# A mixture-of-experts attention stage: deviation by a square root on ScalarE, residual through TensorE, experts' scores on all partitions

## The reference

```
t = transpose(x, (1, 0, 2))                    # the 32 batch entries are the tokens here: s_len = 32
scores = softmax(t @ Wg)                       # over the 16 experts
idx = top_k(scores over the 32, cap = 32 // 16 = 2)      # two tokens of each column for each expert
hg = gather(t, idx)
q, k, v = hg @ Wq + bq, hg @ Wkv + bkv         # heads of 64
att = (q . k) / 8                              # 2 x 2 scores for each of the 256 columns
p = softmax(att, axis=1)                       # over the 256 columns
ao = (p . v) @ Wo + bo
outs = zeros.at[tokens].add(ao)
y = t + outs
yn = (y - mean) * rsqrt(var + 1e-5) * ln_g + ln_b
x = layernorm(x + yn)                          # the decoder's own residual and norm
```

## Time and profile before

| | |
|---|---|
| median of 3 runs | 3803.97 us (3803.84 to 3806.27) |
| the profiled execution | 3800.63 us |
| its span, first to last instruction | 3797.8 us |
| busy, share of the span | TensorE 87%, VectorE 82%, ScalarE 74%, GpSimd 68% |
| mean granted clock of TensorE | 0.95 of 2.4 GHz |
| stage "route" | about 821 to 924 us |
| stage "expert" | 924 to 1054 us |
| stage "scatter" | 1054 to 1204 us, next stage from 1212 us |

### The profile page before, as it was taken

The page is one execution under the profiler, slowest core; times in us unless marked ns, Lnnn a source line. Parts: engine busy times, 40 slices in busy tenths (PEclk is TensorE's granted clock), DMA queues, the critical chain, the costliest instruction groups (busy, mean ns, idle before and its releaser), DMA issues. The chain is left out here.

```text
span 3797.8 us, 75246 instructions
## 1 busy us (share of the span) xinstructions
PE 3290.3 (87%) x23328; PEld 2494.5 (66%) x23360; DVE 3118.3 (82%) x5163; ACT 2817.2 (74%) x5141; POOL 2567.5 (68%) x2971
## 2 busy tenths in 40 slices
PE   8996988979963688999988989898899879997887
PEld 5664666668542477777767777777777757775565
DVE  5665999955386699999899989989999849998887
ACT  2222777854475799899898998989899737776887
POOL 1222767730086599888888988898898936665676
PEclk9998999979976899999999999999999989998999
DMA  2112222242213111121111211111111112322111
GB/s 61 55 55 56 44 53 49 50 106 46 52 34 85 37 52 57 50 54 53 54 53 56 57 50 57 49 53 56 55 52 51 48 47 68 77 54 64 51 61 45
DMA packets 285549, 209.62 MB, mean 55 GB/s; under 512 B 131416, under 2 KB 249752, under 8 KB 285224
## 3 DMA queue, kind: packets, MB, share of 16 engines
q1 hardware_dynamic: 285224, 205.72, 19.9%
HBM read 149.18 MB, written 51.41 MB: 53 GB/s over the span
## 5 line engine op out<-in xcount | busy, mean ns | idle before, releaser
L2896 POOL TENSOR_TENSOR ma_ch<-ma_h,ma_crep 128x512 f32<-128x512 f32 x1024 | 1348.2, 1340 | 190.5 <-DVE ma_h L3007 159.8
L3007 DVE TENSOR_TENSOR_SCAN ma_h<-ma_a,ma_pbu 128x512 f32<-128x512 f32 x1024 | 1196.5, 1203 | 123.5 <-PE ma_pbu L2576 108.1
L2576 PE MATMUL ma_pbu<-ma_ident,ma_bu 128*128 128x128 f32 x4096 | 655.6, 284 | 120.6 <-DVE ma_h L3007 92.6
L2576 PEld LDWEIGHTS ma_pbu<-ma_ident,ma_bu 128*128 128x128 f32 x4096 | 481.5, 144 | 349.2 <-DVE ma_h L3007 204.3
L2785 ACT ACTIVATE ma_a<-ma_dt,ma_A 128x510 f32<-128x510 f32 x1024 | 672.8, 711 | 1.3 <-issue 1.3
L2585 PE MATMUL ma_py<-ma_ident,ma_ch 128*128 128x128 f32 x4096 | 623.9, 278 | 9.8 <-DVE ma_gT L3025 7.8
L2778 ACT ACTIVATE ma_bu<-ma_uT,ma_b_t 128x512 f32<-128x512 f32 x864 | 555.6, 711 | 13.0 <-PE ma_pbu L2576 11.3
L2585 PEld LDWEIGHTS ma_py<-ma_ident,ma_ch 128*128 128x128 f32 x4096 | 493.4, 145 | 14.3 <-DVE ma_gT L3025 11.4
L1576 POOL TENSOR_TENSOR xa_prob<-xa_e,xa_rec_head 128x616 f32<-128x616 f32 x128 | 155.6, 1217 | 126.4 <-DVE xa_rec_head L1668 114.2
L924 POOL TENSOR_TENSOR xa_prob<-xa_e,xa_rec_head 128x616 f32<-128x616 f32 x128 | 155.7, 1217 | 107.0 <-DVE xa_rec_head L1016 90.4
L362 POOL TENSOR_TENSOR la_veps<-la_mv,la_eps 128x2 f32<-128x2 f32 x32 | 6.3, 196 | 248.8 <-DVE la_mv L395 248.8
(11 more groups left out here) (375 smaller groups left out, 7942.3 us busy)
## 6 DMA issues: line engine op xcount, KB each, us to landing
ma_crep<-ma_ct_dram SPq DMA_DIRECT2D x256, 256.0 KB
xa_x<-act SPq DMA_DIRECT2D x64, 256.0 KB, 2.7
act<-xa_y SPq DMA_DIRECT2D x64, 256.0 KB, 2.2
la_x<-in_x SPq DMA_DIRECT2D x32, 256.0 KB, 2.8
act<-la_y SPq DMA_DIRECT2D x32, 256.0 KB
act<-ea_x SPq DMA_DIRECT2D x32, 256.0 KB, 4.0
ma_x<-act SPq DMA_DIRECT2D x16, 512.0 KB, 4.5
ma_xr<-act SPq DMA_DIRECT2D x16, 512.0 KB
```

What stands on the lines that cost most here:

```text
L2576: last = pe.transpose(pbu[c % 2][:, t * P:(t + 1) * P], bu[:, s % 2, t, c * P:(c + 1) * P], ident[:, :])
L2896: pool.tensor_tensor(ch[:, s % 2, c], h[:, s % 2, c], crep[:, s % 4, :], ALU.mult).then_inc(multiplied, 1)
L3007: dve.tensor_tensor_scan(out=h[:, s % 2, c, :], data0=a[:, s % 2, c, :], data1=pbu[c % 2][:, :], initial=0.0, op0=ALU.mult, op1=ALU.add).t ...
```

## The change

In "expert", `sums` becomes a 128 x 128 matrix with ones in two blocks of 64 x 64, set by VectorE instead of being loaded, so that one matmul of 512 columns gives every partition the sum over its half: the score of (i, k) lies on all 64 partitions of i. `pick`, `spread` and `pb` go. The maximum is now over 128 x 2 x 256, the exponential is two instructions of 128 x 256 with a sum each, the reciprocal is 128 x 2, and the normalisation is taken into the multiplication by v (two `scalar_tensor_tensor`). `pa` is doubled.

In "scatter", the residual is added in PSUM by a matmul of the identity with the two tiles of x, ahead of the scattering matmul; `first` and `r` go, `py` has three buffers, and the moments and z read it in PSUM. ScalarE makes the deviation by a square root (`deviation`, at the head of its round) into PSUM, VectorE takes its reciprocal twice, as `rstd` in SBUF for ScalarE and as `factor` in PSUM for the shift. GpSimd's power and addition of epsilon go. A table set with the square root is loaded at the start of the stage.

```diff
-        sums = outer.sb("sums", [P, 2, P])
-        pick = outer.sb("pick", [4, 2, 2, F])
+        sums = outer.sb("sums", [P, P])
...
-                          (sums[halves[i], :, :], sum4_d[:, 2 * i:2 * i + 2, :]),
-                          (pick[:, :, i, :], pick4_d[:, 2 * i:2 * i + 2, 0:F]),
...
                 def attend(e):
                     pe.wait_ge(prod_ready, e + 1)
-                    for k in range(2):
-                        last = pe.matmul(pa[:, :], sums[:, k, :], prod[:, e % 2, k, :], start=(k == 0), stop=(k == 1))
-                    last.then_inc(att_made, 1)
-
-                def spread(e):
-                    pe.wait_ge(prob_ready, e + 1)
-                    at_least(pe, av_ready, e)
-                    for k in range(2):
-                        last = pe.matmul(pb[:, k, :], pick[:, k].rearrange("p h f -> p (h f)"), prob[:, e % 2, :],
-                                         start=True, stop=True)
-                    last.then_inc(spread_made, 1)
+                    at_least(pe, exp_done, e - 1)
+                    pe.matmul(pa[e % 2][:, :, :].rearrange("p k s -> p (k s)"), sums[:, :],
+                              prod[:, e % 2].rearrange("p k s -> p (k s)"), start=True, stop=True).then_inc(att_made, 1)
...
+                pe.wait_ge(sums_ready, 1)
...
                 for e in range(E):
-                    spread(e)
...
                 def expo(e):
                     act.wait_ge(max_ready, e + 1)
-                    act.activation(prob[:, e % 2, :], pa[0:4, :], ACT.Exp, bias=nmax[:, e % 2:e % 2 + 1],
-                                   accum_out=rsum[:, e % 2:e % 2 + 1]).then_inc(exp_done, 1)
+                    for k in range(2):
+                        last = act.activation(prob[:, e % 2, k, :], pa[e % 2][:, k, :], ACT.Exp, bias=nmax[:, e % 2, k:k + 1],
+                                              accum_out=rsum[:, e % 2, k:k + 1])
+                    last.then_inc(exp_done, 1)
...
-                def softmax(e):
+                def largest(e):
+                    dve.wait_ge(att_made, e + 1)
+                    dve.tensor_reduce(nmax[:, e % 2, :], pa[e % 2][:, :, :], AX.X, ALU.max, negate=True).then_inc(max_ready, 1)
+
+                def weigh(e):
                     q = e % 2
-                    dve.wait_ge(att_made, e + 1)
-                    dve.tensor_reduce(nmax[:, q:q + 1], pa[0:4, :], AX.X, ALU.max, negate=True).then_inc(max_ready, 1)
                     dve.wait_ge(exp_done, e + 1)
-                    link(dve.reciprocal(rsum[:, q:q + 1], rsum[:, q:q + 1]))
-                    dve.tensor_scalar(prob[:, q, :], prob[:, q, :], rsum[:, q:q + 1], None, ALU.mult).then_inc(prob_ready, 1)
-
-                def weigh(e):
-                    dve.wait_ge(spread_made, e + 1)
                     dve.wait_ge(v_ready, e + 1)
-                    link(dve.tensor_tensor(pv[:, :, :], pb[:, :, :], v_sb[:, e % 2], ALU.mult))
-                    dve.tensor_tensor(av[:, e % 2, :], pv[:, 0, :], pv[:, 1, :], ALU.add).then_inc(av_ready, 1)
+                    link(dve.reciprocal(rsum[:, q, :], rsum[:, q, :]))
+                    for k in range(2):
+                        last = dve.scalar_tensor_tensor(out=pv[:, k, :], in0=prob[:, q, k, :], scalar=rsum[:, q, k:k + 1],
+                                                        in1=v_sb[:, q, k, :], op0=ALU.mult, op1=ALU.mult)
+                    link(last)
+                    dve.tensor_tensor(av[:, q, :], pv[:, 0, :], pv[:, 1, :], ALU.add).then_inc(av_ready, 1)
 
                 link = Chain(dve, chain, 0)
+                link(dve.memset(sums[:, :], 0.0))
+                for i in range(2):
+                    last = dve.memset(sums[halves[i], halves[i]], 1.0)
+                last.then_inc(sums_ready, 1)
...
                 for e in range(E):
-                    weigh(e)
                     if e + 2 < E:
                         queries(e + 2)
                     if e + 1 < E:
-                        softmax(e + 1)
+                        largest(e + 1)
+                        weigh(e + 1)
                     if e + 2 < E:
                         products(e + 2)
...
-            py = [ps(f"py{k}", [P, 2, D]) for k in range(2)]
+            py = [ps(f"py{k}", [P, 2, D]) for k in range(R)]
+            small = ps("small", [P, 2, 2, 4])
+            std, factor = small[:, 0], small[:, 1]
...
                 def scatter(k):
                     p = k % 2
-                    pe.wait_ge(turn_copied, k + 1)
-                    at_least(pe, res_added, k - 1)
+                    at_least(pe, z_ready, k - R + 1)
                     for t in range(2):
-                        last = pe.matmul(py[p][:, t, :], turned[:, p, t, C, :],
-                                         turned[:, p, t, 0:C, :].rearrange("p c d -> p (c d)"), start=True, stop=True)
+                        pe.matmul(py[k % R][:, t, :], ident[:, :], x[:, 2 * k + t, :], start=True, stop=False)
+                        if t == 0:
+                            pe.wait_ge(turn_copied, k + 1)
+                        last = pe.matmul(py[k % R][:, t, :], turned[:, p, t, C, :],
+                                         turned[:, p, t, 0:C, :].rearrange("p c d -> p (c d)"), start=False, stop=True)
                     last.then_inc(y_made, 1)
...
+                def deviation(n):
+                    act.wait_ge(var_ready, n + 1)
+                    act.activation(std[:, n % 2, :], mv[:, n % 2, :, 1], ACT.Sqrt, bias=eps[:, 0:1]).then_inc(std_ready, 1)
+
...
+                act.preload_act_table_set("sqrt_and_others")
...
                 for k in range(BUNDLES + 1):
+                    n = k - 1
+                    if k >= 1:
+                        deviation(n)
                     if k + 3 < NU:
                         stage(k + 3)
                     if k + 2 < NU:
                         copy(k + 2)
                     if k >= 1:
-                        n = k - 1
                         act.wait_ge(shift_ready, n + 1)
                         if n < NU:
-                            normalise(z[:, n % 2], r[:, n % R], n, 0, z_ready)
+                            normalise(z[:, n % 2], py[n % R], n, 0, z_ready)
...
-                        pool.wait_ge(var_ready, n + 1)
-                        at_least(pool, y_ready, n - 4)
-                        link(pool.tensor_tensor(veps[:, n % 2, :], mv[:, n % 2, :, 1], eps[:, :], ALU.add))
-                        pool.tensor_tensor(rstd[:, n % 2, :], veps[:, n % 2, :], minus_half[:, :], ALU.pow).then_inc(rstd_ready, 1)
...
-                def first(k):
-                    dve.wait_ge(y_made, k + 1)
-                    at_least(dve, z_ready, k - R + 1)
-                    dve.tensor_tensor(r[:, k % R], py[k % 2][:, :, :], pair_tiles(k), ALU.add).then_inc(res_added, 1)
...
-                        dve.wait_ge(res_added, k + 1)
-                        last = moments(r[:, k % R], k, 0)
+                        dve.wait_ge(y_made, k + 1)
+                        last = moments(py[k % R], k, 0)
                     if k >= 1:
                         n = k - 1
-                        dve.wait_ge(rstd_ready, n + 1)
+                        dve.wait_ge(std_ready, n + 1)
+                        dve.reciprocal(rstd[:, n % 2, :], std[:, n % 2, :])
+                        link(dve.reciprocal(factor[:, n % 2, :], std[:, n % 2, :]))
                         dve.scalar_tensor_tensor(out=shift[:, n % 2, :], in0=mv[:, n % 2, :, 0], scalar=-1.0,
-                                                 in1=rstd[:, n % 2, :], op0=ALU.mult, op1=ALU.mult).then_inc(shift_ready, 1)
+                                                 in1=factor[:, n % 2, :], op0=ALU.mult, op1=ALU.mult).then_inc(shift_ready, 1)
```

43 lines of the change are left out of this document (18 added, 25 removed).

## The result

The changed kernel takes 3750.45 us in the median of four executions (3742.73 to 3752.01); the kernel before, run beside it, 3803.9. The ratio, of the means of the two sets, is 0.9855, with an interval of 0.9838 to 0.9872, a gain of 1.45%.

The account below looks back on a forecast made before the run. TensorE was taken to bound the expert stage, VectorE and GpSimd the scatter stage. Expert -17.9 and scatter -25.3 (1.6 - 24.5 - 2.4) make -43.2 us, from a median of 3803.97 to 3761; range 3750 to 3766 (57%).

Parts of the forecast that it names:

- each mark that the prediction named: Gapless TensorE at 6.7 us per expert; scatter: shift 0.2, ScalarE never idle, bundle 3.45, one added table load, clock near 1.0.
- its term for 28 bundles at 3.45 us: Scatter stage, first to last z: 28 bundles on ScalarE at 3.45 us, 96.6 us in all, where each took 4.25.
- Its bound of 3.3: Scatter stage: the low bound for the bundle, 3.3 us, giving -29 us instead of -24.5.
- the 8.4 us of the sum: Scatter stage: the first three bundles, bound by TensorE's 2.8 us each, 8.4 us where they took 10.5.
- a head of 3.0: Scatter stage's head: 3.0 us added instead of 1.6, if a table switch costs a drain of about 1.38 us beside its load.
- The 15 rounds without `spread`: Expert stage: `spread` leaves TensorE's bound 15 times at 1.05 us, -15.8 us.
- The 0.1 us per `attend`: Expert stage: one matmul of 512 columns instead of two of 256 saves 0.1 us each, 1.5 us in 16.
- not 4.25: Expert stage's tail: the last expert from `attend` to `output` takes 4.25 us instead of 5.15, -0.9 us.
- A: Scatter stage: the VectorE-GpSimd port sets the bundle, `second` waiting up to 1.26 us; 3771 to 3782 us; chance 19%.
- B: Scatter stage: the shift still waits for GpSimd despite its input in PSUM; +18 us, 3779 us; chance 6%.
- C: Scatter stage: TensorE's clock stays low; 3768 us at 0.76 (8%), 3820 at 1.2 GHz (4% together with D).
- D: Scatter stage: ScalarE's table sets alternate, two loads per bundle; +87 us, 3848 us; 4% together with C at half clock.

Follow-up runs that it names:

- e1: The kernel before with only the expert part of the change, the scatter stage being the old one; 3780.85 us, ratio 0.9951.
- e4: The changed kernel with the residual added by VectorE into SBUF again and no identity matmuls, the root staying on ScalarE; 3778.32 us, ratio 0.995.
- e3: The changed kernel with epsilon's addition and the power back on GpSimd and the shift reading SBUF, the residual staying on TensorE; 3776.52 us, ratio 0.9941.
- e11: The changed kernel with the sums set in the routing and the square root's table loaded behind the second last expert's output; 3746.68 us, ratio 0.9864.
- e9: The changed kernel, unaltered, run and profiled once more; 3746.16 us, ratio 0.9869 to the kernel before.
- e5: The changed kernel with the shift reading rstd in SBUF and no reciprocal into PSUM; 3754.19 us in one execution.
- e7: The changed kernel with one more memset of 128x256 on VectorE per bundle, behind the first moments; 3749.5 us in one execution.
- e6: The changed kernel with one more square root of four elements on ScalarE per bundle; 3753.56 us in one execution.
- e10: The changed kernel with the three memsets of the sums moved into the routing and TensorE's wait for them dropped; 3747.69 us, ratio 0.9873.
- e8: The changed kernel without ScalarE's staging (experts' results laid out by bundle), with sums set and table loaded early; 3737.2 us, ratio 0.9825.

## Why the prediction was right and wrong

**The mechanism was right.** TensorE stays the bound of the experts, ScalarE becomes the bound of the scattering, the shift falls to 0.16 us, one table load is added, and the clock rises; each mark that the prediction named is in the traces, but for the 3.45 us of the bundle. The failing step is a size: the scatter stage gave 31.4 us where the sum had 25.3, for the most part because its term for 28 bundles at 3.45 us was too high. That difference of 6.1 is what the profiled spans (49.3 against 43.2) differ by; the rest came to 17.9 as forecast, but by chance in part, since a routing shorter by 3.6 us, in which the clock rose earlier, stands against some 2.6 us that the lower clock added to the expert stage (115.2 us where e1 took 112.6).

**The bundle in steady state, the largest miss.** The sum took 3.45 us, the trace has 3.33. It had ScalarE's old work at 3.33, which is 4.26 less the idle time, and added 0.12 for the root: a price of 0.20 read off, less some overlap. The root takes 0.19 in full. Two old terms were too high instead. The first is z, which reads PSUM now. Its pair takes 0.90 us to the next start, where the pair that reads SBUF took 0.99 (1117.44 to 1118.43 in the earlier trace rows and its neighbour). e4, whose z reads SBUF again, has 0.99 (1106.13 to 1107.12), and e3, whose z reads PSUM, 0.91. The second is the pair of copies, behind which the kernel before had its idle time:

```profile
1119.93 0.84 ACT L2228 ACTIVATE scatter_turned<-scatter_pt 128x384 f32<-128x384 f32 x2
```

This pair counts with its whole record, 0.84 us, where the next instruction can't start yet. In the full stream z starts 0.74 behind it (1104.54 to 1105.28). So 3.33 + 0.19 - 0.09 - 0.10 = 3.33: the added root costs nothing on balance. Time less idle time overstates an engine whose instructions overlap, and a term whose source has changed isn't an old term. Its bound of 3.3 was the right end. Over 24 steady bundles that is 24 x 0.12 = 2.9 us.

**The last four bundles.** The sum ran all 28 at the steady value. ScalarE's staging for bundle k+3 ends with k = 28, and so do later the copies, and the last four distances of z are shorter:

```profile
1135.27 1.45 ACT L2236 ACTIVATE scatter_z<-scatter_py,scatter_shift,scatter_rstd 128x256 f32<-128x256 f32 x2
...
1138.37 1.18 ACT L2236 ACTIVATE scatter_z<-scatter_py,scatter_shift,scatter_rstd 128x256 f32<-128x256 f32 x2
...
1141.20 1.02 ACT L2236 ACTIVATE scatter_z<-scatter_py,scatter_shift,scatter_rstd 128x256 f32<-128x256 f32 x2 [0.52 <-DVE scatter_shift L2306]
...
1144.10 1.02 ACT L2236 ACTIVATE scatter_z<-scatter_py,scatter_shift,scatter_rstd 128x256 f32<-128x256 f32 x2 [0.74 <-DVE scatter_shift L2306]
...
1146.77 1.02 ACT L2236 ACTIVATE scatter_z<-scatter_py,scatter_shift,scatter_rstd 128x256 f32<-128x256 f32 x2 [0.52 <-DVE scatter_shift L2306]
```

From 1135.27 to 1146.77 there are four bundles in 11.50 us, where 4 x 3.45 is 13.80: 2.3 more. Brackets come back here, released by the shift: without its staging ScalarE is no longer the bound. While VectorE and GpSimd were the limit, this end saved nothing; whoever makes an engine the bound must run its list of work to the last round. The first three bundles took 2.38, 3.10 and 2.91, the 8.4 us of the sum.

**Head and tail.** The head cost 0.9 to 1.2 us instead of 1.6, since the table load lies half beside other work (e11). The row of the load and the staging behind it in the changed kernel, and a load of the kernel before, in the Mamba stage, between two ACTIVATEs:

```profile
1035.98 1.28 ACT L2240 ACT_TABLE_LOAD   x1 [0.76 <-PEq L40]
1037.27 1.15 ACT L2219 ACTIVATE scatter_slots<-ea_hg 128x512 f32<-128x512 f32 x2
```

```profile
1239.15 0.60 ACT L2711 ACTIVATE ma_sz<-ma_py 128x512 f32<-128x512 f32 x1 [1.12 <-PE ma_py L2683]
1239.77 1.28 ACT L2727 ACT_TABLE_LOAD   x1
1241.07 1.91 ACT L2727 ACTIVATE ma_xc<-ma_xc 128x2048 f32<-128x2048 f32 x1
```

The drain that the prediction cites from the Trainium skill ("ScalarE: Activation LUTs", What ACT_TABLE_LOAD costs) isn't seen: the ACTIVATE starts with the end of the load in both, in the second without idle time ahead of the load either, and a head of 3.0 didn't come. The row of the kernel before could have settled this ahead of the change. From the last z to the last y it took 6.4 us instead of 9.3, a gain of 2.9 against 2.4 forecast; from there to the next stage it took 0.3 longer than before. So the 6.1 us are 2.9 and 2.3 of the bundles, 0.7 of the head and 0.5 of the tail, less that 0.3.

**The expert stage came out right, by errors that cancel.** e1 has 17.54 us less between its marks, and the gap ahead of the first query is 0.49 us longer; net 17.05, against 17.9. The 15 rounds without `spread` gave what was said, 16.0 us. The 0.1 us per `attend` did not come: 1.06 us as one matmul or as two, so the 0.15 that it takes beyond 0.91 doesn't belong to the number of matmuls. The last expert took 4.54 us from `attend` to `output`, not 4.25. What made up for most of the 1.5 us of `attend` was not in the sum at all: the last `output` group of e1 ran at the full clock, 1.13 us (at 1036.90), where the kernel before and the changed kernel took 2.08 (1050.24 and 1031.83) at a granted clock of 0.50. In two of the executions the stage was longer than 112.6 us: 114.3 in e9, because the first keys and values ran at the lower clock (1.7 us), and 115.2 in the changed kernel, which had both that and the slow last `output`. The changed kernel's row, with the 1.98 us of the earlier trace rows for the same four records to hold against it:

```profile
921.82 3.36 PE L2021 MATMUL expert_pk<-ea_hg,ea_wk 128*128 128x512 f32 x4
```

**Rivals.** A falls for this kernel, since `second` meets a quiet GpSimd, and stands in e4. The same hold-up falls on the shift in every other bundle of e5. B falls: the shift takes 157 ns, 159 at most, beside a busy GpSimd. C falls: clock 1.00. D falls: one load.

**The distance that is left.** Of the 12 us between 3761 and 3748.8, 6 are the scatter stage. The rest belongs to no stage's term. The forecast put a profiled run 3.3 us below the median, and in the changed kernel's set it was 0.01 us from it (3750.44 against 3750.45). 0.9 is the part of the profiled run's time outside its span, and 1.6 is the distance of that run from the 3748.8 that the ratio of the means gives. And the kernel before had medians of 3796.4 to 3803.9 us in the sets shown, so its starting value was at the high end. Over both sets of the changed kernel the gain is 50 to 53 us, of which the two stages' marks give 48.5 (17.05 in e1 and 31.43).

**What stays open.** In both profiles of the changed kernel, and in e7, the routing was 1.2 to 3.6 us shorter than in the kernel before, because TensorE's clock rose earlier in it. Here the windows of the routing, kernel before and then the changed kernel, TensorE busy throughout in both:

```profile
846.00:856.00 10.00, 10.00 (x49) 10.00 (x50) 4.01 (x13) 2.64 (x5) 0.00 (x0) 0.50 1.13 224
856.00:866.00 10.00, 10.00 (x66) 10.00 (x66) 5.00 (x16) 3.67 (x7) 0.00 (x0) 0.70 0.78 125
```

```profile
846.00:856.00 10.00, 10.00 (x59) 10.00 (x58) 4.38 (x14) 3.19 (x6) 0.00 (x0) 0.60 1.13 226
856.00:866.00 10.00, 10.00 (x93) 10.00 (x93) 6.83 (x22) 5.14 (x11) 0.00 (x0) 1.00 0.80 123
```

e1, e3, e4, e5 and e6 have the same routing code as the changed kernel and show 98.4 to 98.6 us, so the edit alone does not do it. The expectation of 97 to 99 us for e9 was a miss all the same. In both executions 1.7 us of the gain came back at the head of the expert stage: routing and expert stage together took 209.6 and 209.8 us, and 209.3 (e7) to 211.2 in the others of this expert stage but for e10, e11 and e8, which have the sums early (210.4 to 210.6). What sets the moment of the rise wasn't found, nor why the last `output` ran at the full clock in some executions and not in others.

## What to carry to other kernels

Two edits that give 2 and 3 us alone can give 31 together when each leaves another bound in place (GpSimd's own list in e3, `second` behind the multiply in e4); test them in a two-by-two before one is thrown away. When a change makes another engine the bound, price all of that engine's instructions anew, by the distance of starts and not by its time less its idle time (a source that moves from SBUF to PSUM counts too), and follow its list to the last round. A tiny instruction with two SBUF inputs on VectorE can cost a whole 1.2 us beside GpSimd, and moving one of its inputs to PSUM takes that away; when the bound lies with ScalarE, take a copy away next, as e8 did, and look which engine fills up then.

## What was not expected of the hardware

The delay between VectorE and GpSimd is decided by starts that lie 0.1 us apart (e5), so it can alternate from round to round; and it acts on GpSimd as well, whose additions took 1.73 instead of 1.27 us in e4. A table load between two ACTIVATEs takes 1.29 to 1.30 us from its start to the next, with no drain to be seen. A pair of ACTIVATEs of 128x256 costs ScalarE 0.90 us from PSUM and 0.99 from SBUF. A square root of four elements costs 0.19 us in a full ScalarE stream, though the same rows show it as 0.25 to 0.70 us long. Records of overlapped instructions stretch in this way while ScalarE is the bound: only the distance of starts gives their price.
